# A four-layer graph kernel: turning probabilities and attention columns through a scratch tensor instead of on TensorE

## The chip, the cores and the metric

One core of one Trainium2 chip runs the kernel. The metric is the device time of one execution in microseconds (us); lower is better. A batch has 64 graphs, and everything below that is called "per graph" happens 64 times.

## The reference

`x` is (64, 256, 256): 64 graphs of 256 nodes with 256 features, and one adjacency mask `adj` (256, 256) for all of them. Each layer computes `x = layernorm(x + layer(x))`. All in float32.

```python
# layer 0
e = leaky_relu((x @ W1) @ (x @ W2).T); p = softmax(where(adj > 0, e, NEG)); y = relu(p @ (x @ W3))
# layer 1
h = x @ W; e = leaky_relu((h @ a1)[:, None] + (h @ a2)[None, :]); y = elu(softmax(masked e) @ h)
# layer 2: relu(x @ mlp1 + b1) -> attention like layer 1 without mask, 512 wide (W_fc, a_fc)
#          -> elu + residual -> relu(@ mlp2 + b2) -> attention with mask (W_hand, a_hand) -> elu + residual -> relu
# layer 3: q, k, v projections, 4 heads of 64, masked softmax of q k^T / 8, @ v, @ wo + bo
```

## The kernel before, in words

A matrix of 256 rows lies as two tiles of 128 partitions. Products keep float32 accuracy by splitting each operand into a high part (a rounded copy) and a low part (the rest) and adding three products, so one 256x256x256 product is 12 matmuls (`product3`, L224). The high part is a copy on ScalarE (ACT, L472), the low part a subtraction on VectorE (DVE, L692) or GpSimd (POOL, L991).

The program is one hand-made software pipeline. Each engine has a list of steps in `ORDERS`, each with a stage; in round k the engine walks its list and does each step for graph k minus its stage. The lists fix the order in which each engine takes its work; semaphores connect the engines. A step is named by a letter and a layer: on PE `a3` is the probability-times-values product of layer 2's second attention, on ACT the `elu` work on its result, on DVE `c3` the next operation on that. SP (SyncE) issues every DMA, in the order of its own list, and stands still where a DMA's semaphore isn't there yet.

What the change touches:

- **Turning the probabilities.** Softmax rows lie on partitions, and the following product needs them turned. In layers 0, 1 and 2 PE does this with 4 float32 `transpose` matmuls each against an identity (`transposes`, L240, steps `t0`, `t1`, `t3`) into PSUM; ACT and DVE split the result.
- **Attention columns.** Layers 1 and 2 need one column of h along the free axis of all partitions. `spread` (L246, steps `f1`, `f3`, `f2`, and `b2` for the denominators `rdc`) does it by transposing a broadcast column, 2, 2, 4 and 2 matmuls.
- **o3T** (the input of layer 2's second attention, kept for its residual) is turned back by 4 transposes (step `o3`).
- **Denominators of the unmasked attention.** `d2` (L360) makes 8 matmuls with the probabilities as weights and two columns of ones.
- **Layer 3 already turns through memory.** DVE transposes 32x32 blocks (`x40`, `x42`, L950: STREAM_TRANSPOSE `p<-p`), SP sends the tile to a scratch tensor in HBM (`o40`, `o42`, L200) and fetches it back in four DMAs with the blocks permuted (`i40`, `i42`, L208: `p4T<-scratch`). PE's `a4` (L456) waits for both halves.
- **Start.** SP issues all weights, then `adj` and `ident`; PE and DVE wait for all of it, make the derived columns and split all weights; then `made` lets the pipeline begin.

Of the kernel before, what the change touches and what calls it, by code (L numbers as in the profile page):

```python
# [4 lines left out]
P = 128  # L5
# [15 lines left out]
def run(engine, steps, B):  # L21

    order = parse(ORDERS[engine])
    assert sorted(n for n, _ in order) == sorted(steps)
    for k in range(B + max(s for _, s in order)):
        for name, s in order:
            if 0 <= k - s < B:
                steps[name](k - s)


def graph_stack(nc, x, xT, adj, ident_d, weights, out):
    fp32 = mybir.dt.float32
# [22 lines left out]
    with ExitStack() as ctx:  # L55
# [5 lines left out]

        KEPT = ("b1", "b2", "bq", "bk", "bv", "bo", "m1", "a1", "ahand", "afc")
# [8 lines left out]
        ones = sb("ones", [P, 2])  # L71
        ones2 = sb("ones2", [P, 2], f32r)
# [8 lines left out]
        def small(name, *shape):  # L81
# [40 lines left out]
        o4T = qT  # L122
# [22 lines left out]
        adj_sb = xn1[1][:, :, :].bitcast(i32)
# [5 lines left out]
        names = """loaded made wsplit setup_pe setup_dve setup_pool  # L151
 x0T_in x0_in x0Th x0Tl g0_mm g0h g0 h0_mm h0h h0 s0_mm raw0 nmax0 pro0 rden0 proT0_mm proT0h proT0 av0_mm act0 y0 mv0 rstd0 xn0 xnT0_mm xnT0h xnT0
 h1_mm h1h h1 f1_mm raw1 nmax1 pro1 rden1 proT1_mm proT1h proT1 av1_mm act1 cl1 q1 y1 mv1 rstd1 xn1 xnT1_mm xnT1h xnT1
 o1_mm o1T o1Th o1Tl hfc_mm hfch hfc f2_mm fmax lrow ef u pfc pfch pfcl d2_mm rdc b2_mm rdb v2_mm w2_mm att ex1 cut2 ex2 res o2 o2Th o2T
 o3_mm o3T o3Th o3Tl h3_mm h3h h3 f3_mm raw2 nmax2 pro2 rden2 proT2_mm proT2h proT2 av3_mm act2 cut3 ex3 cl3 q3 on3_mm r3 y2 mv2 rstd2 xn2 xnT2_mm xnT2h xnT2
 q4_mm qTh qT k4_mm kTh kT v4_mm v4 sc4_mm nmx4 p4 rd4a rd4 p4n p4x p4out0 p4out1 p4T0 p4T1 av4_mm o4Th o4T xb4 y4_mm y3 mv3 rstd3 xn3 stored0 stored1""".split()
        S = {n: ctx.enter_context(nc.semaphore("s_" + n)) for n in names}
        stored = [S["stored0"], S["stored1"]]
        p4out, p4Tin = [S["p4out0"], S["p4out1"]], [S["p4T0"], S["p4T1"]]
        block = ctx.enter_context(nc.Block())  # L160

        def by_quads(row):
            return row.rearrange("p (b w j) -> p w b j", b=CT, w=QUADS)

# [5 lines left out]
        n_loads = len(weights) - 2 + 2 + HT + 2  # L170

        @block.sync
        def _(sp):
            for n, w in weights.items():
                if n not in ("fc", "fc_T"):
                    sp.dma_start(W[n][:, :, :], w).then_inc(S["loaded"], 16)
            for i in range(2):
                sp.dma_start(fc_halves[i], weights["fc"][:, 2 * i:2 * i + 2, :]).then_inc(S["loaded"], 16)
# [935 lines left out]
```

## Time and profile before

| | |
|---|---|
| median of 3 runs | 2921.91 us (2917.68 to 2927.56) |
| the profiled execution: its own time | 2918.28 us |
| its span, first to last instruction | 2916.5 us |
| PE busy (matmul) | 2689.4 us, 92% |
| DVE, ACT, POOL busy | 2278.2, 1998.7, 1556.0 us (78, 69, 53%) |
| DMA engines, mean busy share | 22.7% |
| mean granted TensorE clock | 0.983 of full speed |

Busy time is the union of an engine's instructions; matmuls overlap, so the mean duration of one matmul (some 280 ns) is more than the distance between two starts (some 120 ns). In a row of the timeline the first number is the start, the second the time from the first start to the last end, and `xN` says how many instructions of one kind were merged. "SPq" rows are the issuing of a DMA, not its transfer. In the chain of waits, a "DMA" piece is time from an issue until the data's semaphore came.

### The profile page before, as it was taken

The page shows a single profiled execution, that of the slowest core. Times are in us where ns is not written, and L with a number is a line of the kernel's source. Part 1 is how long each engine was busy: PE and PEld are TensorE (multiplying, and loading weights), DVE is VectorE, ACT ScalarE, POOL GpSimd, SP SyncE. Part 2 cuts the span into 40 slices and gives each one's busy share as a digit, 9 for nine tenths or more (in the row PEclk, how much of TensorE's full clock was granted, in tenths as well). Part 3 has the DMA queues.
Part 4 walks back from the last instruction along what each step waited for, and adds up shares of the span by engine and source line. Part 5 has one row for each costly group of instructions (what it writes and reads, how often), then busy time and mean ns, then how long its engine had stood idle before and what let it go on. Part 6 is the DMA issues. An engine that isn't in the chain of part 4 may idle for free.

```text
span 2916.5 us, 61536 instructions
## 1 busy us (share of the span) xinstructions
PE 2689.4 (92%) x22472; PEld 2551.3 (87%) x22472; DVE 2278.2 (78%) x6124; ACT 1998.7 (69%) x4801; POOL 1556.0 (53%) x2119
## 2 busy tenths in 40 slices
PE   4689999999999999999999999999999999999974
PEld 4589999999999999998999998999999999998863
DVE  3257888888888888888888887888888888888874
ACT  1357777777777776777777777777777777776752
POOL 0235555555555555555556555555655555555542
PEclk9799999999999999999999999999999999999997
DMA  3001222222122122212212221221222122122222
GB/s 109 19 16 37 77 81 64 57 81 80 41 80 81 59 63 80 74 47 81 80 51 71 81 72 49 81 81 48 74 81 70 52 80 80 41 81 73 66 66 73
DMA packets 132766, 195.17 MB, mean 67 GB/s; under 512 B 14832, under 2 KB 97136, under 8 KB 132464
## 3 DMA queue, kind: packets, MB, share of 16 engines
q1 hardware_dynamic: 132464, 191.24, 22.7%
q8 instruction: 178, 2.92, 0.4%
q14 instruction: 124, 1.02, 0.1%
HBM read 107.30 MB, written 83.89 MB: 66 GB/s over the span
## 4 chain that ended last, share of the span: by engine, by line
PE 60%; DMA 13%; ACT 8%; SPq 8%; DVE 6%; issue 4%; POOL 1%; POOLq 0%; DVEq 0%
PE ps L224 29%; DMA p4T<-scratch 10%; PE ps L378 6%; SPq L208 6%; PE ps L240 5%; PE ps L436 4%; PE ps L337 4%; PE ps L233 3%; PE ps L338 3%; DMA scratch<-p 3%; DVE p L950 3%; PE ps L456 2%; ACT p L671 2%; PE ps L360 2%; DVE h_lo L692 1%
## 5 line engine op out<-in xcount | busy, mean ns | idle before, releaser
L1067 POOL TENSOR_TENSOR p<-p,rd 128x512 f32<-128x512 f32 x256 | 269.8, 1054 | 20.0
L671 ACT ACTIVATE p<-p,nmx 128x256 f32<-128x256 f32 x512 | 255.7, 504 | 25.4 <-DVE nmx L935 25.2
L991 POOL TENSOR_TENSOR o1Tp_lo<-o1T,o1Tp_hi 128x1024 fp32r<-128x1024 f32 x64 | 153.8, 2403 | 220.8 <-ACT o1Tp_hi L472 220.8
L1003 POOL TENSOR_SCALAR xn<-act,nmean,rstd 128x256 f32<-128x256 f32 x384 | 243.6, 643 | 18.3 <-POOL rstd L998 11.2
L456 PE MATMUL ps<-p4T,v 128*64 128x256 f32 x1024 | 144.3, 404 | 118.2 <-DMA p4T<-scratch 117.7
L995 POOL TENSOR_TENSOR vare<-mv,eps 128x2 f32<-128x2 f32 x256 | 108.0, 422 | 270.5 <-DVE mv L748 270.5
L1060 POOL TENSOR_TENSOR rd<-some,den 128x2 f32<-128x2 f32 x256 | 53.5, 209 | 354.6 <-DVE den L944 354.6
L456 PEld LDWEIGHTS ps<-p4T,v 128*64 128x64 f32 x1024 | 67.3, 140 | 178.1 <-DMA p4T<-scratch 96.5
L692 DVE TENSOR_TENSOR xnT_lo<-ps,xnT_hi 128x512 fp32r<-128x512 f32 x192 | 132.1, 688 | 114.2 <-ACT xnT_hi L472 114.2
L935 DVE CUSTOM_DVE_ANT_0 p<-ps,mask 128x256 f32<-128x256 f32 x512 | 189.9, 418 | 33.3 <-PE ps L436 33.3
L480 ACT ACTIVATE sco<-sco,nmax 128x256 f32<-128x256 f32 x384 | 191.0, 500 | 28.9 <-DVE nmax L736 28.9
L991 POOL TENSOR_TENSOR x0Tp_lo<-x0T,x0Tp_hi 128x512 fp32r<-128x512 f32 x64 | 112.7, 1761 | 162.4 <-ACT x0Tp_hi L472 162.4
L472 ACT ACTIVATE h_hi<-ps 128x512 fp32r<-128x512 f32 x192 | 114.7, 597 | 112.9 <-PE ps L233 98.6
L998 POOL TENSOR_TENSOR rstd<-vare,mhalf 128x2 f32<-128x2 f32 x256 | 179.7, 702 | 0.0
L736 DVE CUSTOM_DVE_ANT_0 sco<-ps,mask 128x256 f32<-128x256 f32 x384 | 146.4, 417 | 40.0 <-ACT ps L475 40.0
L475 ACT ACTIVATE ps<-ps,cols 128x256 f32<-128x256 f32 x384 | 154.5, 441 | 33.7 <-PE ps L246 33.1
L612 ACT ACTIVATE o3T<-ps,b2m 128x256 f32<-128x256 f32 x128 | 53.8, 471 | 171.3 <-PE ps L378 171.3
L337 PE MATMUL ps<-w_fc_lo,o1Tp_hi 128*128 128x258 f32 x512 | 154.8, 302 | 8.5 <-POOL o1Tp_lo L991 5.9
L692 DVE TENSOR_TENSOR h_lo<-ps,h_hi 128x512 fp32r<-128x512 f32 x192 | 131.1, 683 | 38.4 <-ACT h_hi L472 38.4
L742 DVE BATCH_NORM_STATS2 stat<-act 128x6 f32<-128x256 f32 x384 | 143.4, 414 | 19.9 <-POOL act L1013 14.6
L950 DVE STREAM_TRANSPOSE p<-p 128x1024 f32<-128x1024 f32 x128 | 157.4, 1230 | 0.7 <-POOL p L1067 0.7
L224 PE MATMUL ps<-pfcp_lo,hfc_hi 128*128 128x256 f32 x512 | 155.6, 304 | 2.1 <-ACT rdb L472 2.1
(248 smaller groups left out, 12683.1 us busy)
## 6 DMA issues: line engine op xcount, KB each, us to landing
scratch<-p SPq DMA_DIRECT2D x128, 512.0 KB, 2.9
p4T<-scratch SPq DMA_DIRECT2D x512, 128.0 KB, 3.9
x0T<-in_xT SPq DMA_DIRECT2D x64, 256.0 KB, 4.6
x<-in_x SPq DMA_DIRECT2D x64, 256.0 KB, 3.7
out<-xn SPq DMA_DIRECT2D x64, 256.0 KB, 3.0
o1T<-in_mlp SPq DMA_DIRECT2D x1, 512.0 KB, 4.4
p<-in_mlp SPq DMA_DIRECT2D x1, 512.0 KB, 4.5
att<-in_fc SPq DMA_DIRECT2D x1, 512.0 KB, 5.4
```

What stands on the lines that cost most here:

```text
L224: ins = nc.tensor.matmul(dst[:, m, :], lhs[a][:, k, (off + m) * P:(off + m + 1) * P], rhs[b][:, k, :], start=(k == 0 and i == 0), stop=(k ...
L337: nc.tensor.matmul(ps[:, 4, 0:C2], lhs, WP["fc"][b][:, k, 0:C2], start=(k == 0 and i == 0), stop=(k == HT - 1 and i == 2))
L456: ins = nc.tensor.matmul(bank[6][g * HD:(g + 1) * HD, c, :], v4[:, k, h * HD:(h + 1) * HD], p4Tv[:, c, g, k, :, :, :], start=(k == 0), sto ...
L480: ins = nc.scalar.activation(sco[i][:, m, :], sco[i][:, m, :], ACT.Exp, scale=-1.0, bias=nmax[i][:, m:m + 1], accum_out=den[i][:, m:m + 1])
L671: ins = nc.scalar.activation(rows_, rows_, ACT.Exp, scale=-1.0, bias=nmx4[:, h, m:m + 1], accum_out=den4[:, h, m:m + 1])
L692: return V.tensor_tensor(pair[1][:, :, :], whole, pair[0][:, :, :].bitcast(fp32), ALU.subtract)
L935: ins = V.tensor_tensor_reduce(p4v[h // 2][:, h % 2, m, :, :, :].rearrange("p w b j -> p w (b j)"), bank[7 - h % 2][:, m, :].rearrange("p ...
L950: V.transpose(p4[c][:, :, :], p4[c][:, :, :]).then_inc(S["p4x"], 1)
L991: return G.tensor_tensor(lo, whole, hi.bitcast(fp32), ALU.subtract)
L998: G.tensor_tensor(rstd[i][:, :], vare[i][:, :], mhalf[:, :], ALU.pow).then_inc(s_rs, 1)
L1003: ins = G.tensor_scalar(xn[:, m, :], y[:, m, :], nmean[i][:, m:m + 1], rstd[i][:, m:m + 1], ALU.add, ALU.mult)
L1067: G.tensor_tensor(rows_, rows_, rd4[:, h, :].unsqueeze(2).unsqueeze(3).broadcast_to([P, NT, QUADS, CT * QP]), ALU.mult).then_inc(S["p4n"], 1)
```

## The change

1. **Probabilities through scratch.** In the three layers PE's transposes go. DVE transposes 32x32 blocks of the probabilities (`turn`, steps `t0`, `t1`, `t3`) into the tile `act`; SP writes it to `scratch_pro` and reads it back with four DMAs (`o0/i0`, `o1/i1`, `o3/i3`); ACT takes the high part of what came back and POOL (formerly DVE) the low part.
2. **Columns through scratch.** The columns are written by DMAs of single 4-byte elements to `scratch_at` (`r1`, `r3`, `r2`) and read back broadcast to 128 partitions (`f1`, `f3`, `f2`). Scores are then made in SBUF, not in PSUM.
3. **o3T through scratch** in the same way (`o5`, `i5`), and added by DVE in two instructions.
4. **d2** makes 4 matmuls with a 128x128 tile of ones as weights, which give the denominators on all partitions; DVE takes the reciprocal of 128x256 directly, and the spreading of `rdc` goes with its copy on ACT.
5. **Load order.** Layer 0's weights, the first `xT` and `adj` are loaded and split first; the other weights are issued behind them, and split by DVE (with small matmuls on PE) before the first step that uses them (`before` in `run`).
6. **Tiles and banks.** Some tiles are single instead of double (`xn3`), products use other PSUM banks (`enter` keeps one tenant per bank), layer 3's normalisation moves from DVE to POOL, and all five orders are new. The highest stage on PE falls from 9 to 8.

```diff
 ORDERS = {
-    "sp": "lt:0 o40:7 st:9 o42:7 lx:1 i40:7 i42:7",
+    "sp": "r2:5 f2:5 st:9 o5:6 r3:6 o1:3 lx:1 f3:6 lt:0 i1:3 o3:6 o0:1 i3:6 i0:1 i5:6 o40:7 r1:2 o42:7 f1:2 i40:7 i42:7",
...
+            def pro_out(i):
+                def step(t):
+                    sp.wait_ge(S[f"pro{i}_x"], t + 1)
+                    wait(sp, S[f"pro{i}_dma"], back(t - 1))
+                    sp.dma_start(scratch_pro[i].rearrange("p w n -> p (w n)"), flat(act[i])).then_inc(S[f"pro{i}_dma"], 16)
+                return step
+            def pro_in(i):
+                def step(t):
+                    sp.wait_ge(S[f"pro{i}_dma"], sent(t))
...
+                    for w in range(QUADS):
+                        sp.dma_start(rows_[w * QP:(w + 1) * QP, :, :], scratch_pro[i][:, w, :].rearrange("(q j) n -> j q n", q=QUADS)).then_inc(S[f"pro{i}_dma"], 16)
+                return step
...
+            def at_out(i):
+                def step(t):
+                    sp.wait_ge(S[f"at{i}"], t + 1)
+                    wait(sp, S[f"at{i}_dma"], back(t - 1, 1))
+                    sp.dma_start(scratch_at[i].rearrange("m p -> p m"), cols[i][:, :, 1], allow_slow_non_contiguous=True).then_inc(S[f"at{i}_dma"], 16)
+                return step
+            def at_in(i, tile, before):
+                def step(t):
+                    sp.wait_ge(S[f"at{i}_dma"], sent(t, 1))
+                    wait(sp, *before(t))
+                    sp.dma_start(tile[:, :, 0, :], scratch_at[i].unsqueeze(0).broadcast_to([P, NT, P])).then_inc(S[f"at{i}_dma"], 16)
+                return step
...
-            def t0(t):
-                pe.wait_ge(S["pro0"], t + 1)
-                transposes(bank[0], sco[0]).then_inc(S["proT0_mm"], 1)
...
-            def f1(t):
-                pe.wait_ge(S["h1"], t + 1)
-                spread(ps[:, 1, 0:N], lambda m: cols[1][:, m, 1:2]).then_inc(S["f1_mm"], 1)
...
             def d2(t):
                 pe.wait_ge(S["pfcl"], t + 1)
-                for m in range(NT):
-                    for k in range(NT):
-                        for i in (1, 0):
-                            ins = nc.tensor.matmul(ps[:, 5, 2 * m:2 * m + 2], pfcp[i][:, k, m * P:(m + 1) * P], ones2[:, :],
-                                                   start=(k == 0 and i == 1), stop=(k == NT - 1 and i == 0))
+                enter(5, "rdb", t + 1)
+                for k in range(NT):
+                    for i in (1, 0):
+                        ins = nc.tensor.matmul(ps[:, 5, 0:N], ones2[:, :], pfcp[i][:, k, :], start=(k == 0 and i == 1), stop=(k == NT - 1 and i == 0))
...
             def t0(t):
-                ac.wait_ge(S["proT0_mm"], t + 1)
-                copy(proT[0][0][:, :, :], bank[0]).then_inc(S["proT0h"], 1)
+                ac.wait_ge(S["pro0_dma"], back(t))
+                wait(ac, S["av0_mm"], t)
+                high_of_turned(proT[0], 0).then_inc(S["proT0h"], 1)
...
             def e1(t):
                 dv.wait_ge(S["raw1"], t + 1)
-                masked(1, lambda m: ps[:, 1, (1 - m) * N:(2 - m) * N]).then_inc(S["nmax1"], 1)
+                masked(1, lambda m: sco[1][:, :, m, :]).then_inc(S["nmax1"], 1)
...
             def t1(t):
-                dv.wait_ge(S["proT1h"], t + 1)
-                low_part(proT[1], bank[1]).then_inc(S["proT1"], 1)
+                dv.wait_ge(S["pro1"], t + 1)
+                wait(dv, S["xn1"], t)
+                turn(1).then_inc(S["pro1_x"], 1)
...
             def f2(t):
-                dv.wait_ge(S["f2_mm"], t + 1)
-                V.reduce_max(fmax[:, :], ps[:, 4, N:2 * N], AX.X).then_inc(S["fmax"], 1)
+                dv.wait_ge(S["at2_dma"], back(t, 2))
+                V.reduce_max(fmax[:, :], row2[:, 1, :], AX.X).then_inc(S["fmax"], 1)
...
-            po.wait_ge(S["made"], 1)
```

How the orders move work is seen in the built programs. Here is one round of the end of SP's queue, before (`p_0`, `p_1` are layer 3's two tiles of probabilities):

```order
L200 DMA scratch<-p_0 128x1024
L194 DMA out<-xn_1 128x2x256
L200 DMA scratch<-p_1 128x1024
L190 DMA x<-in_x 128x512
L208 DMA p4T<-scratch 32x4x256 x8
L186 DMA x0T<-in_xT 128x512
```

and one whole round after the change, 40 DMAs where there were 13 (`scratch_pro` carries the probabilities of layers 0 to 2, `scratch_at` the columns, `scratch_o` the turned o3T):

```order
L277 DMA scratch_at<-cols 128x4x1
L283 DMA row<-scratch_at 128x2x128 x2
L227 DMA out<-xn 128x2x256
L249 DMA scratch_o<-sco 128x512
L263 DMA scratch_at<-cols 128x2x1
L234 DMA scratch_pro<-act 128x512
L223 DMA x<-in_x 128x512
L271 DMA sco<-scratch_at 128x2x128
L217 DMA x0Tp<-in_xT 128x512
L243 DMA sco<-scratch_pro 32x4x128 x4
L234 DMA scratch_pro<-act 128x512 x2
L243 DMA sco<-scratch_pro 32x4x128 x8
```

The rest of that round of SP's queue, with layer 3's turn at its end (`p4T` is what `a4` on PE reads):

```order
L256 DMA o3r<-scratch_o 32x4x128 x4
L289 DMA scratch<-p_0 128x1024
L263 DMA scratch_at<-cols 128x2x1
L289 DMA scratch<-p_1 128x1024
L271 DMA sco<-scratch_at 128x2x128
L297 DMA p4T<-scratch 32x4x256 x8
```

Between the second write of layer 3's turn and its fetches the load of `x` has made room for a column's fetch (`f1`), whose write (`r1`) stands two places ahead; each fetch in the list waits for its own write to land.

On DVE, the place around the second transposition of layer 3's probabilities, before:

```order
L885 TENSOR_SCALAR act<-act 128x512 [waits s_act2]
L944 RECIPROCAL den<-den 128x2 [waits s_p4]
L950 STREAM_TRANSPOSE p_0<-p_0 128x1024 [waits s_p4n]
L889 TENSOR_SCALAR act<-act 128x512 [waits s_ex3]
L692 TENSOR_TENSOR h_lo<-ps,h_hi 128x512 [waits s_h0h]
L950 STREAM_TRANSPOSE p_1<-p_1 128x1024 [waits s_p4n]
```

and after:

```order
L992 TENSOR_TENSOR att<-ex,att 128x1024 [waits s_res,s_ex2]
L953 COPY cols<-ps 128x2 [waits s_ef,s_hfch]
L956 TENSOR_TENSOR hfc_lo<-ps,hfc_hi 128x512
L908 COPY cols<-ps 128x4 [waits s_raw1,s_h1h]
L788 TENSOR_TENSOR h_lo<-ps,h_hi 128x512
L1026 TENSOR_SCALAR act<-act 128x512 [waits s_act2]
L1095 STREAM_TRANSPOSE p_1<-p_1 128x1024 [waits s_p4n]
```

Only `c3` (`act<-act`, which waits for ACT's work on PE's `a3`) now stands directly ahead of the transposition; the first tile's transposition has moved further up, and h's low part of layer 0 away.

## Rows read from the trace of the kernel before

**Rows 1.** The page: busy us (share of the span) and instructions of each engine.
```profile
PE 2689.4 (92%) x22472; PEld 2551.3 (87%) x22472; DVE 2278.2 (78%) x6124; ACT 1998.7 (69%) x4801; POOL 1556.0 (53%) x2119
```
**Rows 2.** Windows (busy us, count of PE, PEld, DVE, ACT, POOL; clock, DMA share, GB/s).
```profile
0.00:100.00 100.00, 50.89 (x214) 46.47 (x215) 28.62 (x75) 14.72 (x32) 9.17 (x20) 0.83 0.27 85
...
1000.00:1400.00 400.00, 385.23 (x3279) 367.51 (x3278) 327.81 (x897) 291.87 (x709) 228.06 (x312) 1.00 0.23 66
```
**Rows 3.** Timeline of SP's queue: two stores 52 graphs apart, and eight fetches.
```profile
376.66 0.43 SPq L194 DMA_DIRECT2D out<-xn  x1
...
1575.05 4.02 SPq L208 DMA_DIRECT2D p4T<-scratch  x8
...
2593.87 0.43 SPq L194 DMA_DIRECT2D out<-xn  x1
```
**Rows 4.** Chain of waits in order of time, one round (start, us, what).
```profile
1540.97 1.08 PE ps L456 x8
...
1568.59 0.47 ACT act L640
...
1572.88 1.16 DVE p L950
...
1582.93 1.08 PE ps L456 x8
```
**Rows 5.** Timeline of PE: transposes, a product's pace, the column sums.
```profile
1501.98 0.60 PE L240 MATMUL ps<-ident,sco 128*128 128x128 f32 x4
1502.42 0.60 PE L240 MATMUL ps<-ident,xn 128*128 128x128 f32 x4
...
1504.27 0.28 PE L378 MATMUL ps<-o2T_lo,w_mlp_hi 128*128 128x256 f32 x1
...
1507.12 0.28 PE L224 MATMUL ps<-h_lo,proT_hi 128*128 128x256 f32 x1
...
1519.21 0.27 PE L360 MATMUL ps<-ones,pfcp_lo 128*128 128x2 f32 x1
...
1520.12 0.66 PE L240 MATMUL ps<-ident,xn 128*128 128x128 f32 x4
```
**Rows 6.** Groups of instructions by line, DVE, POOL and ACT (busy us, mean ns | idle).
```profile
L950 DVE STREAM_TRANSPOSE p<-p 128x1024 f32<-128x1024 f32 x128 | 157.4, 1230 | 0.7 <-POOL p L1067 0.7
...
L692 DVE TENSOR_TENSOR gT_lo<-ps,gT_hi 128x512 fp32r<-128x512 f32 x128 | 87.6, 684 | 32.5 <-ACT gT_hi L472 32.5
...
L902 DVE SCALAR_TENSOR_TENSOR act<-act,xn 128x512 f32<-128x512 f32 x64 | 70.1, 1096 | 0.0
L972 DVE TENSOR_SCALAR xn<-xn,nmean,rstd 128x256 f32<-128x256 f32 x128 | 66.9, 562 | 1.1 <-POOL rstd L998 1.1
L885 DVE TENSOR_SCALAR act<-act 128x512 f32<-128x512 f32 x64 | 57.2, 894 | 21.4 <-ACT act L640 21.3
...
L898 DVE TENSOR_TENSOR act<-act,ps 128x512 f32<-128x512 f32 x64 | 44.0, 688 | 7.0 <-DVE act L801 0.5
...
L640 ACT ACTIVATE act<-ps,rden 128x256 f32<-128x256 f32 x128 | 53.8, 472 | 52.4 <-PE ps L224 52.4
...
L1003 POOL TENSOR_SCALAR xn<-act,nmean,rstd 128x256 f32<-128x256 f32 x384 | 243.6, 643 | 18.3 <-POOL rstd L998 11.2
...
L991 POOL TENSOR_TENSOR pfcp_lo<-pfc,pfcp_hi 128x512 fp32r<-128x512 f32 x64 | 82.5, 1288 | 20.8 <-ACT pfcp_hi L472 20.8
```
**Rows 7.** DMA: the queue, and issues (KB each, median us from issue to landing).
```profile
q1 hardware_dynamic: 132464, 191.24, 22.7%
...
scratch<-p SPq DMA_DIRECT2D x128, 512.0 KB, 2.9
p4T<-scratch SPq DMA_DIRECT2D x512, 128.0 KB, 3.9
...
w_a<-in_a SPq DMA_DIRECT2D x1, 2.0 KB, 4.5
```
**Rows 8.** Timeline of the start: PE's first matmuls, and the first of layer 0.
```profile
23.29 3.78 PE L252 MATMUL ps<-p4T 128*128 128x256 f32 x8 [23.29 <-DMA ident<-in_ident]
...
45.16 0.55 PE L224 MATMUL ps<-x0Tp_lo,A_hi 128*128 128x256 f32 x1 [4.65 <-POOL x0Tp_lo L991]
```

More of the change, by code:

```diff
@@ L18, in parse, with run @@
     return [(name, int(stage)) for name, stage in (x.split(":") for x in text.split())]
-def run(engine, steps, B):
+def run(engine, steps, B, before={}):
     order = parse(ORDERS[engine])
@@ L27, in run @@
             if 0 <= k - s < B:
+                if k == s and name in before:
+                    before[name]()
                 steps[name](k - s)
@@ L163, in by_quads, with by_tiles, flat, sent @@
             return row.rearrange("p (b w j) -> p w b j", b=CT, w=QUADS)
+        def by_tiles(row):
+            return row.rearrange("p (b n) -> p b n", b=CT)
+        def flat(tile):
+            return tile[:, :, :].rearrange("p a n -> p (a n)")
+        def sent(t, n=QUADS):
+            return 16 * (n + 1) * t + 16
+        def back(t, n=QUADS):
+            return 16 * (n + 1) * (t + 1)
         def wait(eng, sem, n):
@@ L172, in _ @@
+        LOADS = (("W1T", "W2T", "W3"), ("W_T", "a1", "W_"), ("mlp1", "b1", "afc", "mlp2", "b2", "hand", "hand_T", "ahand", "m1"), ("wqT", "bq", "wkT", "bk", "wvT", "bv", "woT", "bo"))
+        n_loads = [len(LOADS[0]) + 1, len(LOADS[1]) + 1, len(LOADS[2]) + 2 + HT, len(LOADS[3])]
         @block.sync
         def _(sp):
[L174 to L178, printed above, removed]
@@ L196, in turn_out, with at2_in @@
+            def at2_in(t):
+                sp.wait_ge(S["at2_dma"], sent(t, 2))
+                wait(sp, S["u"], t)
+                for c in range(2):
+                    sp.dma_start(by_tiles(row2[:, c, :]), scratch_at[2][c::2, :].unsqueeze(0).broadcast_to([P, NT, P])).then_inc(S["at2_dma"], 16)
             def turn_out(c):
@@ L198, in step @@
                     sp.wait_ge(S["p4x"], 2 * t + c + 1)
[L199 to L200 removed]
+                    wait(sp, p4_dma[c], back(t - 1))
+                    sp.dma_start(scratch[c], p4[c][:, :, :]).then_inc(p4_dma[c], 16)
                 return step
@@ L241, in transposes @@
                 return ins
-            def spread(dst, col):
-                for m in range(NT):
-                    ins = nc.tensor.transpose(dst[:, m * P:(m + 1) * P], col(m).broadcast_to([P, P]), ident[:, :])
-                return ins
-            pe.wait_ge(S["loaded"], 16 * n_loads)
+            pe.wait_ge(S["loaded0"], 16 * n_loads[0])
             for m in range(CT):
                 for k in range(CT):
-                    nc.tensor.matmul(bank[0][:, m, :], W["W1T"][:, k, m * P:(m + 1) * P], W["W2T"][:, k, :], start=(k == 0), stop=(k == CT - 1))
@@ L375, in mlp2 @@
-            def mlp2(m):
-                for k in range(HT):
-                    for i, (a, b) in enumerate(PAIRS):
-                        ins = nc.tensor.matmul(bank[3][:, m, :], WP["mlp2"][a][:, k, m * P:(m + 1) * P], o2T[b][:, k, :],
-                                               start=(k == 0 and i == 0), stop=(k == HT - 1 and i == 2))
-                return ins
+                pe.wait_ge(S["pfcl"], t + 1)
+                enter(5, "att", t + 1)
+                product3(half_of(5), hfc, pfcp, NT, 2, off=2).then_inc(S["w2_mm"], 1)
@@ L895, in r3 @@
             def r3(t):
-                dv.wait_ge(S["on3_mm"], t + 1)
+                dv.wait_ge(S["o3_dma"], back(t))
                 dv.wait_ge(S["q3"], t + 1)
-                V.tensor_tensor(act[2][:, :, :], act[2][:, :, :], bank[2], ALU.add).then_inc(S["r3"], 1)
+                for m in range(NT):
+                    row = act[2][:, m, :].rearrange("p (k q c) -> p k q c", k=CT, q=QUADS)
+                    ins = V.tensor_tensor(row, row, o3r[:, :, :, m, :].rearrange("p q k c -> p k q c"), ALU.add)
+                ins.then_inc(S["r3"], 1)
             def z3(t):
```

545 lines of the change are left out of this document (322 added, 223 removed), and 8 rows, old and new, of the table ORDERS.

## The prediction

> **What bounds the kernel now.** I read the busy shares first: PE is busy for 92% of the span, DVE for 78% [rows 1]. An average hides the filling and draining of the pipeline, so next the windows. In the middle of the run PE is busy for 385.23 of 400 us at the full granted clock, DVE for 327.81, ACT for 291.87, POOL for 228.06 [rows 2]. Then the period: the stores at 376.66 and 2593.87 us are 52 graphs apart [rows 3], so one graph takes 2217.21 / 52 = 42.64 us. PE works 385.23 / 400 x 42.64 = 41.07 us of it; DVE 34.9, ACT 31.1, POOL 24.3. So PE is the engine to relieve, but it idles for 1.57 us per graph, and something other than PE sets that.
>
> The chain of waits tells what. It is a loop through all engines that closes once per round [rows 4]: from the start of `a4`'s second half at 1540.97 PE works without a pause until its product `a3` has ended, and ACT starts on it at 1568.59 (27.62 us); ACT's `act` and some ACT and DVE work queued behind it lead to the second block transposition, which ends at 1572.88 + 1.16 = 1574.04 (5.45 us); SP writes the tile out, issues eight fetches in 4.02 us [rows 3], and the last lands when PE starts again at 1582.93 (8.89 us). The sum of this round is 41.96 us; the mean round has 0.68 more, and I put that on the DMA part, 9.57 us.
>
> Outside the 64 periods lie 2916.5 - 64 x 42.64 = 187.5 us: 45.2 until PE's first product of layer 0 [rows 8], and 142.3 for filling and draining. The first 100 us show it, with PE busy for 50.89 [rows 2].
>
> **The change, part by part.** *PE.* Four transposes take 1502.42 - 1501.98 = 0.44 us, 0.11 each; the 24 matmuls of one product pair take 1507.12 - 1504.27 = 2.85 us, 0.119 each [rows 5]. Removed per graph are 12 transposes of probabilities, 8 and 2 of columns, 4 of o3T: 26 x 0.11 = 2.86 us. `d2` took 1520.12 - 1519.21 = 0.91 us [rows 5] and has 4 matmuls of 256 columns now, 0.48: 0.43 less. Some switches between kinds of matmul go, about 0.35. PE's work falls from 41.07 to **37.4 us** per graph. Counted otherwise: 350 matmuls become 320.
>
> *DVE.* It loses three low parts of 0.684, two normalisations of 0.562 and a reciprocal of 2 columns (0.15): 3.3 us. It gains four transpositions of half of the 1.230 us one, 2.5 us, and some 0.5 for a 256-column reciprocal and for `r3` in two instructions [rows 6]. That is 34.1 to 34.6 us. The price that the trace doesn't show directly is what the operations of layers 1 and 2 cost now that both inputs are in SBUF. The sum of two SBUF tiles L902 takes 1096 ns, the one with a PSUM input L898 of the same size 688 [rows 6]. Seven instructions change sides so (four maskings, two of `r3`, one subtraction): 0 to 7 x 0.41 = 2.9 us, so DVE ends between 34.1 and 37.5 us per graph, under the period in each case. The Trainium skill (SBUF — State Buffer, Who interferes with whom) says that a DVE instruction with two SBUF inputs contends with a GpSimd instruction that reads SBUF, and that one blocks for the whole of the other. By that rule L902 is the blocked kind, and DVE's upper bound is the likelier one; the period would stay as it is in my sum.
>
> *POOL* gains three low parts of 1.288 and two normalisations of 0.643 [rows 6]: 24.3 + 5.2 = 29.5 us. *ACT* loses one copy and stays near 31. Both are hidden under PE.
>
> *SP.* 13 issues become 40, at 4.02 / 8 = 0.50 us each [rows 3]: 20.1 us. A fetch that stands close behind its write also waits for the landing of it, 2.9 us at the least [rows 7]: whole for `f2`, some 2 us each for `f3`, `i3` and 1 to 2 for `f1`. SP's own round is about 29 us; it fits.
>
> *The DMA engines.* 2070 packets per graph took 22.7% of 45.6 us, 10.3 us [rows 7]. New are 4 x 640 for the turns, 1024 single elements and 1024 rows of 512 bytes: 6700 packets. At today's time per packet that is 33 us per graph, by bytes (5.6 MB for 3.0) 19 us. So they aren't the bound, but landings may become later.
>
> *The loop after.* Its PE part is the whole round of 37.4 less what PE's list puts between `a3` and the second half of `a4`: 84 matmuls of products, 10.0 us, one turning of 0.44 and half of `a4`, 1.08 [rows 4]. That gives 25.9, and 0.4 for passing on: 26.3 us. Then ACT's two `act` instructions, DVE's `c3` and, directly behind it, the transposition: 2 x 0.472 + 0.894 + 1.230 with some overlap [rows 6], 3.1 us where it was 5.45. The DMA part has the same number of issues (one column fetch for the load of `x`): 9.57 us. The sum is 39.0 us. **Unknown** is what the column's DMA `r1`/`f1` adds, since `f1` stands ahead of the eight fetches and waits for 256 single elements to land, and what the crowded queue adds to the landings. A lower bound is 0. The upper: `r1` lands after 4.5 us like a small load at the start [rows 7] and is covered by a low part, `c3` and the transposition (0.68 + 0.89 + 1.23 = 2.8 us [rows 6]), which leaves 1.7 us; and landings grow from 3.9 by 2.9 us, a whole write's landing: 4.6. I take 1.2, near the lower end, since SP was idle between rounds before, and the loads of the start ran in a denser queue than any round will have. So the period is **40.2 us**, and PE idles for 2.8 of it. The late stretch is still `p4T`, not PE.
>
> *Start, filling and draining.* PE's setup runs from 23.29, and layer 0 begins at 45.16 [rows 8]. Now `adj` is the fifth DMA, issued near 3 us, and lands 4.5 us later like the small load [rows 3, 7], near 7.6; 3.78 us of matmuls and some 2.5 us of copying and splitting follow: 14 us. But the rest of the 22 us of setup is not gone. It stands on DVE and PE ahead of the first steps that need it, and I charge 12 us in the filling. Each graph's way gets longer by three turns (issue, 2.9, four issues, 3.9: 9.3 us) and three columns (7.8 us), 51 us at most; since several stand side by side in a round I take 30, bounds 0 and 51. The shorter period and one PE stage less give back about 12. So 14 + 142 + 12 + 30 - 12 = 186 us, as before.
>
> **Sum:** 64 x 40.2 + 186 = 2759 us of span, 2760 with the 1.8 us by which the profiled execution exceeded its span. That execution was 3.6 us under the median of the runs; I leave this within the rounding.
>
> **The rivals.** *(a) PE alone is the bound.* If landings are as before and the loop is covered, the period is PE's 37.4 and 0.8 of passing on, 38.2: 64 x 38.2 + 175 = 2620. For it: the list was cut so that PE's first half of `a4` covers some landing. Against: the loop of 39.0 is a sum of rows and leaves no room. Chance 0.14, with all down to 2680.
>
> *(b) SP's order becomes a second loop.* DVE's `f2` waits for the columns of `r2`, written, landed, fetched twice and landed again: 0.5 + 2.9 + 1.0 + 3.9 = 8.3 us, where DVE's own work between (about 6.2 us) covers less. DVE then has 34.6 + 2.1, or 37.5 + 2.1 with all two-input operations slow; together with `a4` late, PE's `s40` waits for DVE's `v4`. That makes a period of 41 to 42: 2820 to 2880. Chance 0.17.
>
> *(c) Slower than before.* The single elements land late. From the place of `r1`, every us beyond about 3.5 delays the eight fetches and then `a4` one for one. The period passes 42.6 when `r1` takes some 7 us to land; at 10 us it is 39.0 + 6.5 = 45.5, and the time 3100. Against it: no transfer in the trace took so long, the longest small one 4.5 us [rows 7]; but no transfer in it has 4-byte runs. The skill warns here (DMA: Bandwidth & Descriptors, Specifications: under 512 bytes the engines read, modify and write; VectorE: DVE Perf Modes, The three transpose paths: a plain copy that strides is 19 times slower than the crossbar). No row here shows either. By it the case (c) would hold for `r1`, and my sum would not. Chance 0.10.
>
> *(d) No difference,* by the second loop and the column together: 0.02. That the change doesn't do what it says is excluded by the built orders, where the 26 transposes are gone.
>
> **How the numbers follow.** My case has 0.57 and spans periods of 39.3 to 41.2, 2680 to 2825 us. Two in ten may stay outside: (c), (d) and the slow end of (b), and the fast end of (a). So the range is 2640 to 2860. What can be told from no change is about 0.3%, 9 us. Faster: my case, (a) and (b), 0.88; same 0.02; slower 0.10.
>
> **What would show it.** Stores 40.2 us apart; PE busy for some 37.4 us per graph, and its longest wait again `p4T<-scratch` at `a4`; the chain going PE, ACT `act`, DVE `p`, SP, DMA; the first product of layer 0 near 14 us; DMA share of 45 to 80%; two-input maskings over 417 ns. I am wrong if the chain rests on `scratch_at` or on SP's issuing, if DVE is busy for over 38 us per graph, if PE's idle time per graph is under 1 us, or if filling and draining have grown by more than 50 us.

## The result, and the profile after

The changed kernel took 4371.23 us (median of 4 runs, 4363.39 to 4378.73), the kernel before 2923.60 us on the same chip. The ratio is 1.4954, 95% interval 1.4910 to 1.4997. The prediction was 2760 us, faster. It was wrong by the sign and by 1600 us; the time lies outside its range, and also far above the 3100 us of its slow rival.

First the page of the kernel after: busy us, share and instructions; then the granted clock in tenths; the DMA queue; the chain that ended last, by engine and by line; and DMA issues with KB each and median us to landing.

```profile
PE 2903.4 (67%) x20552; PEld 2648.6 (61%) x20552; DVE 2383.0 (55%) x6124; ACT 1984.7 (45%) x4737; POOL 1950.5 (45%) x2439
...
PEclk7778788888888878888878888888878888878786
...
q1 hardware_dynamic: 455024, 359.38, 37.1%
...
DMA 56%; DVE 12%; PE 9%; POOL 8%; issue 7%; SPq 6%; ACT 2%; DVEq 0%; ACTq 0%; POOLq 0%
DMA scratch_at<-cols 36%; DMA sco<-scratch_at 7%; DMA row<-scratch_at 6%; DMA scratch<-p 6%; PE ps L314 5%; SPq L297 5%; POOL p L1205 5%; PE ps L498 3%; DVE sco L852 2%; POOL x0Tp_lo L1130 2%; DVE p L1095 1%; DVE p L1080 1%; DVE att L978 1%; POOL proT_lo L1130 1%; DMA p4T<-scratch 1%
...
scratch<-p SPq DMA_DIRECT2D x128, 512.0 KB, 9.7
p4T<-scratch SPq DMA_DIRECT2D x512, 128.0 KB, 5.2
```

The first row answers to [rows 1], the DMA rows to [rows 7]. Every engine is idle for a third of the span or more, and the DMA engines work for 37.1% of it. So nothing is full, and yet 56% of the chain is spent between a DMA's issue and its landing. 36% of the chain is one kind of DMA, the single elements of a column. The write `scratch<-p`, which the change did not touch, lands after 9.7 us instead of 2.9.

The window that answers to the second of [rows 2], and the stores at both ends of 53 graphs ([rows 3]):

```profile
1000.00:1400.00 400.00, 268.43 (x1920) 244.17 (x1920) 223.49 (x583) 189.21 (x455) 183.82 (x228) 0.82 0.40 85
```
```profile
526.29 0.46 SPq L227 DMA_DIRECT2D out<-xn  x1
...
3989.47 0.47 SPq L227 DMA_DIRECT2D out<-xn  x1
```

One graph now takes (3989.47 - 526.29) / 53 = 65.34 us, against 42.64. Outside the 64 periods lie 4363.1 - 64 x 65.34 = 181 us, 6 less than before: the whole loss is in the period. The granted clock is 0.82 where it was 1.00, between the two levels of 1.2 and 2.4 GHz, with PE busy for 268 us of 400 where it was 385. I take that for a consequence: PE is idle for a third of each round, and its matmuls are 9% of the chain above, so a slower clock cannot be what costs 22.7 us a graph.

The chain in order of time shows one round (start, us, what):

```profile
2005.29 8.54 DMA scratch_at<-cols
...
2021.18 9.61 DMA scratch_at<-cols
...
2031.23 4.09 DMA row<-scratch_at
2035.87 0.36 SPq L263
...
2045.95 4.37 DMA sco<-scratch_at
2050.75 0.50 ACT sco L543
...
2072.88 9.66 DMA scratch<-p
...
2084.38 11.13 DMA scratch_at<-cols
```

From `r2` to `r2` (2021.18 to 2084.38) pass 63.20 us. `r2`'s 512 elements land after 9.61. `r3` is issued at 2035.87 and its fetch can only be issued at 2045.95, 10.08 later. The fetch lands and ACT starts at 2050.75, 4.80 later. ACT, DVE, PE and POOL work until 2072.88, 22.13 us. Layer 3's write lands after 9.66. What is left, 6.9 us, are the 5.1 between the landing of `r2` and the issue of `r3` (the fetch of `r2`'s column, 4.09, with the DVE work that waits for it) and 1.8 of issuing at the end. `r1`, 8.54 us in the round before, runs beside layer 3's write and holds the fetches up too.

SP's own waits (total us, times, longest) between 1000 and 3000 us, which is 30.6 graphs:

```profile
SPq L271 <- DMA scratch_at<-cols: 391.5, 56, 9.7
SPq L283 <- DMA scratch_at<-cols: 300.0, 30, 11.7
```

So SP's queue, whose round the forecast put at 29 us, stands still for (391.5 + 300.0) / 30.6 = 22.6 us of each round on three column writes alone, and everything listed behind them waits. The three landings themselves add up to 28 us; SP issues other work during a part of them.

### The profile page after: what moved, and what is told of

It is laid out like the page before. It is cut to its first block, busy times and chain, and to the rows that moved or that the text cites. A ratio compares the mean times of both kernels' runs of the same rounds, so it can differ in the third digit from the quotient of the medians.

```text
span 4363.1 us, 63290 instructions
## 1 busy us (share of the span) xinstructions
PE 2903.4 (67%) x20552; PEld 2648.6 (61%) x20552; DVE 2383.0 (55%) x6124; ACT 1984.7 (45%) x4737; POOL 1950.5 (45%) x2439
## 3 DMA queue, kind: packets, MB, share of 16 engines
q1 hardware_dynamic: 455024, 359.38, 37.1%
## 4 chain that ended last, share of the span: by engine, by line
DMA 56%; DVE 12%; PE 9%; POOL 8%; issue 7%; SPq 6%; ACT 2%; DVEq 0%; ACTq 0%; POOLq 0%
DMA scratch_at<-cols 36%; DMA sco<-scratch_at 7%; DMA row<-scratch_at 6%; DMA scratch<-p 6%; PE ps L314 5%; SPq L297 5%; POOL p L1205 5%; PE ps L498 3%; DVE sco L852 2%; POOL x0Tp_lo L1130 2%; DVE p L1095 1%; DVE p L1080 1%; DVE att L978 1%; POOL proT_lo L1130 1%; DMA p4T<-scratch 1%
## 5 line engine op out<-in xcount | busy, mean ns | idle before, releaser
L543 ACT ACTIVATE sco<-sco,cols 128x256 f32<-128x256 f32 x256 | 116.0, 500 | 1087.5 <-DMA sco<-scratch_at 1087.5
L324 PE MATMUL ps<-ident,xn 128*128 128x128 f32 x768 | 174.0, 370 | 623.9 <-ACT o3T L701 437.7
L852 DVE CUSTOM_DVE_ANT_0 sco<-sco,mask 128x256 f32<-128x256 f32 x256 | 98.7, 423 | 883.8 <-ACT sco L543 883.8
L324 PEld LDWEIGHTS ps<-ident,xn 128*128 128x128 f32 x768 | 122.0, 190 | 644.5 <-issue 640.8
L1130 POOL TENSOR_TENSOR proT_lo<-sco,proT_hi 128x512 fp32r<-128x512 f32 x128 | 165.8, 1295 | 698.4 <-ACT proT_hi L540 698.4
L498 PE MATMUL ps<-kT_lo,qT_hi 64*128 64x256 f32 x512 | 112.0, 423 | 483.1 <-DVE v L1073 479.6
L1205 POOL TENSOR_TENSOR p<-p,rd 128x512 f32<-128x512 f32 x256 | 394.6, 1542 | 15.6
L524 PE MATMUL ps<-p4T,v 128*64 128x256 f32 x1024 | 232.7, 619 | 118.3 <-DMA p4T<-scratch 118.2
L314 PE MATMUL ps<-h_lo,proT_hi 128*128 128x256 f32 x512 | 160.1, 313 | 83.9 <-POOL proT_lo L1130 83.9
L540 ACT ACTIVATE xnT_hi<-ps 128x512 fp32r<-128x512 f32 x192 | 114.6, 597 | 146.7 <-PE ps L324 145.1
```

The source lines that it names most:

```text
L314: ins = nc.tensor.matmul(dst(m), lhs[a][:, k, (off + m) * P:(off + m + 1) * P], rhs[b][:, k, :], start=(k == 0 and i == 0), stop=(k == kt ...
L324: ins = nc.tensor.transpose(dst[:, b, a * P:(a + 1) * P], src[:, a, b * P:(b + 1) * P], ident[:, :])
L498: ins = nc.tensor.matmul(bank[7 - g % 2][:, m, :], qT[a][rows_, g // 2, m * P:(m + 1) * P], by_quads(kT[b][rows_, g // 2, :]), start=(i == ...
L524: ins = nc.tensor.matmul(bank[6][g * HD:(g + 1) * HD, c, :], v4[:, k, h * HD:(h + 1) * HD], p4Tv[:, c, g, k, :, :, :], start=(k == 0), sto ...
L852: ins = V.tensor_tensor_reduce(sco[i][:, :, m, :], whole(m), by_tiles(mask16[:, m, :]), -1.0, BIG, ALU.add, ALU.min, nmax[i][:, m:m + 1])
L1130: return G.tensor_tensor(lo, whole, hi.bitcast(fp32), ALU.subtract)
```

## The experiments

Two theories stood against each other at first. **Landing (L):** 256 elements of 4 bytes land late, since the writes of elements that lie side by side in memory wait for one another. **Engines (E):** the DMA engines are loaded by so many small packets. Beside these was **queue (Q)**: other transfers that share the queue with such a write land late too. The expectations of runs 1 and 2 call the late elements theory A, and their theory B puts the time on SP's 40 issues and the doubled traffic.

**1. The same columns as runs of 128 bytes.** A 32x32 block transposition on VectorE puts the column along the free axis of a few partitions first, so that a DMA writes rows of 32 elements instead of single ones.

```diff
-sp.dma_start(scratch_at[i].rearrange("m p -> p m"), cols[i][:, :, 1], allow_slow_non_contiguous=True)...
+for m in range(NT):
+    sp.dma_start(scratch_at[i][m, :].rearrange("(w j) -> w j", j=QP), colsT[i][2 * m + 1::QP, :])...
```

> The changed kernel, but the attention columns are first turned by a 32x32 block transposition on DVE (128x32, three more per graph) and then written in pieces of 128 bytes, not as single elements: 5 more DMAs per graph, 45 instead of 40. Theory A (the single 4-byte elements are late, some 8 to 10 us from issue to landing, and everything behind them waits): the writes land in 2 to 3 us, the period falls from 65 us to 39 to 43, the time to 2700 to 2950 us, and the granted clock returns to 1.0. Theory B (SP's 40 issues and the doubled traffic hold the loop, the elements only a part): the period stays over 52 us, the time over 3500 us.

Measured: 2941.36 us (6 runs), ratio to the kernel before 1.0056 (1.0036 to 1.0076). 1430 of the 1448 us are gone, with the same bytes (359.38 MB), more DMAs, the same fetches and the same order of the lists. Between 1000 and 2000 us the DMA share is 0.45 where it was 0.40, and the granted clock 0.99 where it was 0.82. Theory A holds. Its chain in order of time:

```profile
1503.45 1.52 DMA scratch_at<-colsT
1504.99 3.82 DMA sco<-scratch_at
...
1538.62 1.92 DMA scratch_at<-colsT
...
1540.98 3.77 DMA row<-scratch_at
```

In the chain of 1000 to 2000 us a column's write lands after 1.5 to 3.1 us (33 of them, half under 1.7) instead of 8.5 to 12.1. What remains of the columns is mostly the fetch. In this round the chain runs over `r2`, its fetch, `r3` and its fetch, then over DVE and POOL. This is in kind the second loop of rival (b), which named 41 to 42 us; the stores of this run are 42.97 us apart.

**2. The columns on TensorE again.** `f1`, `f2`, `f3` are steps of PE as before the change. All else of the change stays.

```diff
-    "sp": "r2:5 f2:5 st:9 o5:6 r3:6 o1:3 lx:1 f3:6 lt:0 ...
+    "sp": "st:9 o5:6 o1:3 lx:1 lt:0 ...
-    "pe": "... r2:5 a0:2 ... a4:8 h3:6 ... y4:8 q4:7",
+    "pe": "... r2:5 f1:3 a0:2 ... a4:8 f2:5 h3:6 ... y4:8 f3:6 q4:7",
+            def f1(t):
+                enter(1, "raw1", t + 1)
+                spread(ps[:, 1, 0:N], lambda m: cols[1][:, m, 1:2]).then_inc(S["f1_mm"], 1)
```

> The changed kernel with the columns spread by transposes on PE again (8 matmuls more per graph, 7 DMAs fewer); probabilities and o3T still go through scratch. Theory A: no element DMA, so the period is 39 to 43 us and the time 2680 to 2950 us; PE is busy some 1 us more per graph than in the run with 128-byte pieces. Theory B: 33 DMAs per graph and nearly all traffic stay, so the time stays over 3300 us.

Measured: **2796.06 us**, ratio 0.9566 (0.9550 to 0.9581). This is faster than both kernels. Its window, two stores 53 graphs apart, and its DMA issues:

```profile
1000.00:2000.00 1000.00, 955.84 (x8018) 899.83 (x8017) 913.93 (x2315) 743.46 (x1801) 753.15 (x932) 1.00 0.41 124
```
```profile
351.00 0.43 SPq L227 DMA_DIRECT2D out<-xn  x1
...
2519.22 0.43 SPq L227 DMA_DIRECT2D out<-xn  x1
```
```profile
scratch<-p SPq DMA_DIRECT2D x128, 512.0 KB, 3.0
p4T<-scratch SPq DMA_DIRECT2D x512, 128.0 KB, 3.6
```

The period is 40.91 us, and 178 us lie outside the periods. Landings are as before the change ([rows 7]), although the queue still carries 325.54 MB where it carried 191.24: three turns of probabilities and one of o3T don't crowd it. DMA is 1% of the chain of this version; POOL has 33%, PE 30% and DVE 27%. POOL's part of one round reads:

```profile
1521.19 1.25 POOL x0Tp_lo L1153
1522.44 1.45 POOL p L1228
...
1524.30 1.90 POOL p L1228
1526.21 1.23 POOL proT_lo L1153
...
1527.67 1.90 POOL p L1228
...
1530.84 1.44 POOL gT_lo L1153
...
1538.81 1.11 POOL xn L1165 x2
```

From 1521.19 to 1539.92 nearly all of the way is POOL's, with 3 us of DVE's statistics and `act` in it. The rest of the round goes over PE's products (11 us) and DVE (8 us, 1.76 of them the reciprocal `rdb`), so this is a loop through three engines, and `p4T` is no longer in it.

**3. Each element in 64 bytes of its own.** The same number of 4-byte packets, 64 bytes apart in memory. This run and the next two leave the columns out of the result: what is fetched is constant, wholly here and in run 5, in part in run 4.

```diff
-sp.dma_start(scratch_at[i].rearrange("m p -> p m"), cols[i][:, :, 1], allow_slow_non_contiguous=True)...
+sp.dma_start(scratch_pad[i][:, :, 0].rearrange("m p -> p m"), cols[i][:, :, 1], allow_slow_non_contiguous=True)...
```

> The changed kernel, but each 4-byte element is written to a 64-byte place of its own in a larger scratch tensor; what is read back is another, constant tensor, so the columns are left out of the result. Same number of elements, same waits. Theory L (writes into one 64-byte piece of memory wait for each other, 16 elements in a piece): r1's landing falls from 8 us to under 4, and the time to under 3300 us. Theory E (each element costs its engine the same wherever it goes): landings stay 8 to 10 us and the time 4250 to 4450 us.

Measured: 2891.65 us (one run), 42.3 us per graph. The packets are as many as in the changed kernel, and the DMA share is higher (0.47 where it was 0.40). The first column of a run has little beside it, so the delay from its issue to the issue of its fetch is a measure of the write alone. After the change:

```profile
54.83 0.38 SPq L263 DMA_DIRECT2D scratch_at<-cols  x1
63.03 0.38 SPq L271 DMA_DIRECT2D sco<-scratch_at  x1
```

and with 64 bytes for each element:

```profile
52.98 0.38 SPq L267 DMA_DIRECT2D scratch_pad<-cols  x1
54.56 0.38 SPq L275 DMA_DIRECT2D sco<-scratch_at  x1
```

8.20 us become 1.58. In the filling and draining of the pipeline there are eight such quiet writes, with nothing issued between them and their fetch: 7.97 to 9.67 us after the change, 1.55 to 1.60 here. It is not the number of packets, nor the 4 bytes, nor the strided source, since all of these are the same. It is where the elements lie in memory. Theory E falls.

**4. Half of the elements.** 128 elements side by side in place of 256, and 256 for 512.

```diff
-sp.dma_start(scratch_at[i].rearrange("m p -> p m"), cols[i][:, :, 1], ...
+sp.dma_start(scratch_at[i][0:1, :].rearrange("m p -> p m"), cols[i][:, 0:1, 1], ...
```

> The changed kernel with half of the elements written (one of the two node tiles; the other half of each column is left out and read as constants). Theory L: 8 us remain, since each piece of 64 bytes still gets its 16 elements: time 4200 to 4400 us. Theory E: r1 and r3 land after 5 us, r2 after 7 to 8, the round loses about 10 us: 3600 to 3900 us.

Measured: 4208.47 us (one run), as theory L said. The first column takes 54.96 to 62.62, 7.66 us, for half of the elements; the eight quiet writes take 7.51 to 8.23. So the delay hardly goes by the count of elements. It fits that elements which share a piece of memory wait for one another: half of the elements fill half as many pieces, and each is as full as before. Which size the piece has this run cannot tell, since a full piece of 64 bytes and one of 512 both stay full. That they wait one after another is an inference, not seen in a record.

**5. Four elements in 64 bytes.** Like run 3, but the elements lie 16 bytes apart.

```diff
-... nc.dram_tensor(f"scratch_pad{i}", [c * NT, P, 16], ...
+... nc.dram_tensor(f"scratch_pad{i}", [c * NT, P, 4], ...
```

> The changed kernel with each element 16 bytes from the next, so that 4 stand in 64 bytes instead of 16 (and 1 in the padded run); the columns are left out of the result as there. Theory L with a piece of 64 bytes: each element of a piece adds about (8.2 - 1.6) / 15 = 0.44 us, so r1 lands after 1.6 + 3 x 0.44 = 2.9 us and the time is 2900 to 3050 us. If a piece is 512 bytes, 32 elements share it and r1 lands after 8 us or more, with over 4000 us.

Measured: 2945.06 us (one run), 43.2 us per graph. The time is in the range of theory L, but the first column took 55.83 to 57.41, 1.58 us, where it named 2.9; the eight quiet writes take 1.57 to 2.54. One write in the middle of the run:

```profile
1503.06 2.95 DMA scratch_pad<-cols
1506.03 3.76 DMA sco<-scratch_at
```

The writes of `r3` are the best to compare in the full queue, since SP waits for little else before their fetch. From issue to fetch their median is 9.90 us after the change, 9.33 in run 4, 2.81 here, 1.56 in run 3 and 2.09 in run 1. So closeness costs by degrees, and not evenly. A piece of 64 bytes holds 16 elements when they lie side by side, 4 here and 1 in run 3; a piece of 512 bytes holds 128, 32 and 8. An even price for each element of a 64-byte piece, some 0.5 us from 8.20 / 16, would give about 2 us for 4 of them in the quiet start, and 1.58 is what 1 takes too. What counts as a piece, and what each further element adds, stays open. Only this is excluded: that sharing 512 bytes is enough to be slow. The Trainium skill (DMA: Bandwidth & Descriptors, Specifications) says that below 512 bytes a transfer reads, modifies and writes. That rule made the case (c) of the prediction likelier and pointed the right way. But by it alone runs 1, 3 and 5, with pieces of 128 and 4 bytes, would be slow too, and they aren't: the measurement decides.

**6. The kernel before with single elements ahead of a write.** A DMA of 256 elements, which nobody reads, is issued between the two writes of layer 3's turn.

```diff
-    "sp": "lt:0 o40:7 st:9 o42:7 lx:1 i40:7 i42:7",
+    "sp": "lt:0 o40:7 st:9 rx:7 o42:7 lx:1 i40:7 i42:7",
+            def column(t):
+                sp.wait_ge(S["p4x"], 2 * t + 1)
+                wait(sp, S["x_dma"], 16 * t)
+                sp.dma_start(scratch_x.rearrange("m p -> p m"), ident[:, 0:2], allow_slow_non_contiguous=True)...
```

> The kernel before, with one column of 256 single 4-byte elements written per graph from a constant tile to an own tensor in HBM, right ahead of the second write of layer 3's turn on SP's queue; nothing reads it and only the next such write waits for it. Theory Q (what is behind the elements on the queue lands behind them): the write of p lands after 8 to 10 us instead of 2.9, a4 waits 6 us longer per graph, the time is 3200 to 3400 us. Theory W (only SP's own wait for the elements costs): one issue more, 0.4 us per graph, 2920 to 2960 us.

Measured: 3474.65 us (one run) against 2917.17, 557 us for 64 KB in all. Its DMA issues:

```profile
scratch<-p SPq DMA_DIRECT2D x128, 512.0 KB, 10.7
p4T<-scratch SPq DMA_DIRECT2D x512, 128.0 KB, 4.1
...
x<-in_x SPq DMA_DIRECT2D x64, 256.0 KB, 11.6
```

Nobody waits for the elements, and SP isn't held by them. The write issued 1.75 us behind them now lands after 10.7 us instead of 2.9, and a load after 11.6. Theory Q holds, and it is dearer than the 3200 to 3400 us that it named. The Trainium skill (DMA: Bandwidth & Descriptors, Queues, rings and completion order) says that a transfer's semaphore is raised by a strongly ordered write, which lands only after every earlier write of its DMA engine; the 10.7 and 11.6 us agree. The fetches `p4T<-scratch`, 4.1 us, are issued some 10 us later and don't pay.

**7. The same elements behind the eight fetches.** With nothing urgent behind them.

```diff
-    "sp": "lt:0 o40:7 st:9 rx:7 o42:7 lx:1 i40:7 i42:7",
+    "sp": "lt:0 o40:7 st:9 o42:7 lx:1 i40:7 i42:7 rx:7",
```

> The same elements, but issued behind the eight fetches of p4T, where SP's queue has nothing urgent for some 30 us. Theory Q: nothing that anyone waits for lands behind them, 2915 to 2950 us. Theory W: the same as ahead, 2920 to 2960 us.

Measured: 3012.21 us (two runs), ratio 1.0323 (1.0267 to 1.0380). This is above both expectations, which ended at 2950 and 2960. Most rounds take 42 to 43 us as before, and 13 of the 62 between stores take 46.7 to 51.9. In one of these SP's timeline and then the chain read:

```profile
590.47 4.29 SPq L214 DMA_DIRECT2D p4T<-scratch  x8
594.87 0.38 SPq L200 DMA_DIRECT2D scratch_x<-ident  x1
```
```profile
594.46 9.55 DMA p4T<-scratch
```

The last fetch had been issued 0.41 us before the elements, and landed 9.55 us later. So a transfer that is issued ahead of them and is still under way can pay as well, and theory Q as written, which spared it, was too narrow. Why only in some rounds stays open.

**8. The old column sums in the version of run 2.** `d2` as 8 matmuls with two columns, the reciprocal of 2 columns, and the spreading of `rdc` on PE with its copy on ACT. It asks whether VectorE's reciprocal of 256 columns holds that version.

```diff
-    for i in (1, 0):
-        ins = nc.tensor.matmul(ps[:, 5, 0:N], ones2[:, :], pfcp[i][:, k, :], ...)
+    for i in (1, 0):
+        ins = nc.tensor.matmul(ps[:, 5, 2 * m:2 * m + 2], pfcp[i][:, k, m * P:(m + 1) * P], ones2[:, :], ...)
```

> The run with the columns on PE, with the denominators of the unmasked attention made as before too: 8 matmuls with two columns of ones, a reciprocal of 2 columns, its spreading by 2 transposes on PE and a copy on ACT. The 256-column reciprocal took 1.76 us on DVE in its loop and goes. Theory R (it stands in the loop, between PE's products and POOL's scaling): 1.0 to 1.6 us per graph less, 2695 to 2735 us. Theory P (POOL's scalings and DVE's other work hold the loop, the new hand-overs through PE and ACT give it back): within 0.6% of 2796 us.

Measured: 2872.83 us, ratio 0.9843 (0.9814 to 0.9872). That is 77 us more than run 2, 1.2 us per graph, and both theories missed: R named 2695 to 2735, P 2796 within 0.6%. DVE's share of the chain falls from 27 to 13% and PE's rises from 30 to 46%. With these lists the detour over PE and ACT costs more than the 1.75 us on VectorE that it removes; part 4 of the change earns its place here.

**9. A low part from GpSimd to VectorE in the version of run 2.** The 1.44 us of `gT_lo` (layer 0's turned probabilities) that stand in POOL's stretch go to VectorE, as a step behind its second transposition.

```diff
-    "dv": "c3:7 x42:8 b3:7 ...
+    "dv": "c3:7 x42:8 w0:2 b3:7 ...
-    "po": "... p43:8 t0:2 v4:9 ...
+    "po": "... p43:8 v4:9 ...
```

> The version with the columns spread on TensorE (2796 us), and in it the low part of layer 0's turned probabilities (1.44 us on GpSimd in each graph, within GpSimd's stretch from the low part of x0T over the first scaling of p onwards) is computed by VectorE instead, behind the second half of its turns of the last layer. Theory G (the loop of that version runs over GpSimd's part, which its chain of waits shows): each graph is shorter by between a third and all of the 1.44 us, 2705 to 2765 us. Theory V (VectorE, busy 914 us of 1000 there, takes the loop over with some 1.2 us more): 2790 to 2830 us. PE's work is 37 to 38 us a graph in either.

Measured: 2822.47 us, ratio 0.9699 (0.9682 to 0.9717); run 2's interval is wholly below it. Theory V holds. The new chain says how:

```profile
1502.11 1.04 DVE act L1055
1503.15 1.15 DVE p L1124
1504.30 1.52 DVE gT_lo L972
...
1508.22 4.53 PE ps L314 x36
```

The moved step is itself in the loop, directly behind the transposition. POOL's share of the chain falls from 33 to 14%, DVE's rises from 27 to 34% and PE's from 30 to 42%. PE works 39.1 us a graph, where the text said 37 to 38. I took one place in VectorE's list; another was not tried, so this doesn't show that POOL had no part in run 2's period.

## Why the prediction was wrong, point by point

**The step that failed** is the term "Unknown", what `r1`/`f1` adds: 1.2 us, with bounds of 0 and 4.6. Its upper bound took the landing of a column from a 2 KB load at the start, 4.5 us [rows 7]. That row has the bytes of a column, but not its pattern: 256 pieces of 4 bytes that lie side by side in memory. Measured, `r1` lands after 8.20 us with nothing beside it, and the fetch behind it can be issued only after 8.5 to 11.2 in a round. The text said itself that no transfer in the trace had 4-byte runs, and then gave the case a chance of 0.10.

**Two more errors made rival (c) too cheap.** It charged only what `r1` adds beyond 3.5 us, 6.5 us at a landing of 10 us. (1) All three columns stand in one queue, and each holds SP until its own write has landed. "SP's own round is about 29 us; it fits" counted 2.9 us landings; with 8.5, 9.6 and 10.1 us instead, SP stands still for 22.6 us on columns alone, and the loop runs `r2`, `r3`, layer 3's write, `r2`. (2) Transfers near a column are late too: `scratch<-p` by 6.8 us, and by 7.8 in run 6, where nothing else was changed. So the period passed 45.5 and went to 65.34.

**The other steps,** measured where the columns don't cover them, in run 2:

| per graph, us | predicted | run 2 |
|---|---|---|
| PE's work | 37.4, and 0.9 for 8 column transposes | 39.1 |
| DVE | 34.1 to 37.5 | 37.4 |
| POOL | 29.5 | 30.8 |
| ACT | 31 | 30.4 |
| period | 39.0 without the column's 1.2 (loop over `p4T`) | 40.91 (loop over POOL, PE, DVE) |
| outside the periods | 186 | 178 |

The first product of layer 0 started at 13.32 us in the changed kernel, where 14 was forecast. The rest of the change did make the kernel faster, but by less than the forecast's own sum. Without the column's 1.2 us that sum gives 64 x 39.0 + 186 = 2682 us, and 2740 with 0.9 for the eight transposes; run 2 took 2796. That this lies in the forecast's range, and near its 2760, is luck in part, since the 2760 hold a price for the column that run 2 doesn't pay. The mechanism was wrong too: "the late stretch is still `p4T`" is false in run 2. The cut loop over `p4T` got out of the way, and a loop through POOL, PE and DVE was next, with POOL's scalings and DVE's reciprocal in it dearer than forecast. One smaller slip: the low end of the forecast's own case, 2680 us for a period of 39.3, doesn't follow from its sum, 64 x 39.3 + 186 = 2701.

**Mis-sized terms.** The reciprocal of 256 columns was put, with `r3`, at "some 0.5" us; it takes 1.74 us without `r3`. `c3` went from 0.894 [rows 6] to 1.00 us. GpSimd's scaling `p<-p,rd` went from 1054 to 1542 ns, four times a graph, 1.95 us that the forecast had at nothing. These groups of the kernel after (mean ns behind the busy us):

```profile
L1205 POOL TENSOR_TENSOR p<-p,rd 128x512 f32<-128x512 f32 x256 | 394.6, 1542 | 15.6
...
L971 DVE RECIPROCAL rdb<-ps 128x256 f32<-128x256 f32 x64 | 111.4, 1741 | 1.1 <-PE ps L443 1.1
L852 DVE CUSTOM_DVE_ANT_0 sco<-sco,mask 128x256 f32<-128x256 f32 x256 | 98.7, 423 | 883.8 <-ACT sco L543 883.8
```

**The price of two SBUF inputs** was bounded at 0 to 0.41 us for each instruction. It is neither an even price nor nothing. The maskings take 423 ns above, as little as with a PSUM input; but in run 2 their mean is 658, since in most graphs one of the four takes about 1.47 us. The timelines of DVE and of POOL show what it meets:

```profile
1049.18 1.47 DVE L875 CUSTOM_DVE_ANT_0 sco<-sco,mask 128x256 f32<-128x256 f32 x1
```
```profile
1049.10 1.27 POOL L1153 TENSOR_TENSOR o3Tp_lo<-o3T,o3Tp_hi 128x512 fp32r<-128x512 f32 x1
```

It starts 0.08 us behind an instruction of GpSimd with two SBUF inputs, and ends 0.28 us after it (1050.65 against 1050.37), where alone it takes some 0.42 us. So the price is one collision, paid whole, where the orders happen to meet. The Trainium skill's rule (SBUF — State Buffer, Who interferes with whom) says this: one of the two blocks for the whole of the other. The trace agrees, and the forecast's use of it (every such instruction pays alike, and only VectorE's) was wrong. GpSimd pays as well. Its scaling at 1524.30 in the round of run 2 above takes 1.90 us, and VectorE's timeline has this 0.21 us ahead of it:

```profile
1524.09 1.21 DVE L1010 SCALAR_TENSOR_TENSOR att<-att,o1T 128x1024 f32<-128x1024 f32 x1
```

That is an instruction with two SBUF inputs, and so is the one at 1527.45 (`att<-ex,att`, 1.21 us), 0.22 us ahead of the next scaling of 1.90. The one at 1529.80 starts with no such instruction under way and takes 1.04, as in the kernel before. No run moved these instructions apart, so that the overlap is the cause is read from the timeline and not tested.

**What the prediction had right:** the engines' work within 2 us a graph, the start, filling and draining (181 us, 178 in run 2, for 186), the DMA engines not being the bound, and its own sign that it would be wrong: "if the chain rests on `scratch_at`".

## What to carry to other kernels

Before a small DMA goes on the path, ask where its elements fall in memory as well as how many bytes it has: a column written as 4-byte neighbours landed here after 8 to 12 us, spread out or turned first into rows of 128 bytes after 1.5 to 2.5 in a quiet queue and 1.5 to 5 in a full one. A slow write isn't paid by its reader alone. All transfers close to it are late, so one such DMA of 1 KB can cost 8.7 us of every round, even when nobody reads it. And where a queue waits on landings, add up all the waits of the list before calling it slack; an unshown price in three places of one list counts three times.

## What was not expected of the hardware

- 4-byte writes to neighbouring addresses: 8.20 us for 256 elements and 7.66 us for 128, and 1.58 us for 256 that lie 16 or 64 bytes apart, all in a quiet queue; in a full one 9.90, 9.33, 2.81 and 1.56. Time goes by how close they lie much more than by their number. Most of the effect lies between 4 and 16 bytes; 8 wasn't tried.
- A transfer issued 0.41 us ahead of such a write landed after 9.55 us. Order of issue alone doesn't protect it.
- The reciprocal of 128x256 takes 1.74 us, 6.8 ns a column, where a subtraction of 128x512 takes 0.68.
- A fetch broadcast to 128 partitions takes 3.2 to 5.3 us to land, 3.8 in the median (run 1). So even with a fast write, a column over memory takes about 1.5 + 3.8 = 5.3 us, where two transposes take 0.22 us of PE. Run 1, with two such ways in its chain, is 145 us behind run 2.
